# Attention: the product with the reciprocals moves to GpSimd for twelve chunks, and the maxima change sign in another instruction

## The reference, cut to what matters

```
scores = jnp.einsum('bhqd,bhkd->bhqk', q, k) / jnp.sqrt(jnp.float32(HD))
causal = jnp.tril(jnp.ones((s, s), dtype=bool))
scores = jnp.where(causal, scores, -jnp.inf)
attn = jax.nn.softmax(scores, axis=-1)
y = jnp.einsum('bhqk,bhkd->bhqd', attn, v)
```

## Time and profile before

| | |
|---|---|
| median of 3 runs | 2291.08 us |
| the profiled execution's own time | 2291.7 us |
| its span | 2290.0 us |
| TensorE (PE) busy | 2055.6 us, 90% |
| VectorE (DVE) busy | 1624.2 us, 71% |
| ScalarE (ACT) busy | 1080.5 us, 47% |
| GpSimd (POOL) busy | 715.7 us, 31% |
| attention stage | about 988 to 1720 us of the span |

### The profile page before, as it was taken

How to read it: one execution, slowest core, us unless ns; L and a number is a source line. 1 busy time by engine, 2 the same in 40 slices (tenths; PEclk the granted TensorE clock), 3 DMA queues, 4 the chain that set the end, 5 groups by cost and what they waited for, 6 DMA issues and landing times. The chain is left out here.

```text
span 2290.0 us, 41749 instructions
## 1 busy us (share of the span) xinstructions
PE 2055.6 (90%) x17396; PEld 1211.0 (53%) x17396; DVE 1624.2 (71%) x2564; ACT 1080.5 (47%) x1060; POOL 715.7 (31%) x494
## 2 busy tenths in 40 slices
PE   7899999999995999989998898898992499999998
PEld 3554444444442445544444444444431499999997
DVE  7789999999976566667778778778567544444442
ACT  6688898898861233213434444444430222323331
POOL 3410000000002112325676767767541222222211
PEclk9999999999997999959999999999996699999999
DMA  7321221221215114351022031010213444444431
GB/s 276 136 82 49 69 75 49 74 71 52 74 31 193 37 47 138 134 119 38 20 66 46 19 82 30 19 38 10 79 42 129 156 120 120 120 117 116 118 69 23
DMA packets 91961, 187.95 MB, mean 82 GB/s; under 512 B 14365, under 2 KB 23581, under 8 KB 87389
## 3 DMA queue, kind: packets, MB, share of 16 engines
q1 hardware_dynamic: 82812, 164.30, 21.9%
q0 software_dynamic: 8960, 20.98, 4.9%
HBM read 139.51 MB, written 41.28 MB: 79 GB/s over the span
## 5 line engine op out<-in xcount | busy, mean ns | idle before, releaser
L1475 ACT ACTIVATE t_E<-t_s 128x1024 f32<-128x1024 f32 (+3 forms) x320 | 278.0, 894 | 420.9 <-PE t_s L1700 231.3
L1541 DVE TENSOR_REDUCE t_rm<-t_m 128x1 f32<-128x512 f32 (+3 forms) x640 | 370.4, 603 | 139.7 <-PE t_m L1683 85.9
L615 ACT ACTIVATE m_step<-m_ub,gat_bias 128x2048 bf16<-128x2048 f32 x128 | 250.0, 1989 | 14.2 <-DMA m_ub<-scratch_uac 8.8
L757 PE MATMUL m_bd<-m_mask,m_S 128*32 128x512 bf16 x3072 | 230.3, 379 | 11.0 <-DVE m_mask L705 11.0
L757 PE MATMUL m_bd<-gat_adjT,m_S 128*32 128x512 bf16 x2496 | 201.4, 379 | 4.8 <-PE m_dn L757 4.8
L757 PE MATMUL m_bd<-m_mask,m_neg 128*32 128x512 bf16 x2496 | 188.9, 379 | 0.0
L2056 POOL DMA_INDIRECT out<-e_ye,e_token x40 | 80.9, 2024 | 338.9 <-DVE e_ye L2159 334.2
L942 POOL MEMSET k_triq<- 128x128 bf16 x1 | 0.2, 204 | 574.8 <-POOLq L2281 574.8
L2220 PE MATMUL e_h<-e_xTh,e_w1h 128*128 128x320 f32 x512 | 159.0, 311 | 1.4 <-DVE e_xTl L2140 1.4
L1714 PE MATMUL t_o<-t_E,k_rows 128*32 128x512 f32 (+3 forms) x1280 | 159.7, 573 | 0.5 <-DVE t_out L1501 0.5
L2220 PE MATMUL e_h<-e_xTh,e_w1l 128*128 128x320 f32 x512 | 158.8, 310 | 0.0
(11 more groups left out here) (371 smaller groups left out, 4414.4 us busy)
## 6 DMA issues: line engine op xcount, KB each, us to landing
a_adj<-in_adj SPq DMA_DIRECT2D x16, 1024.0 KB, 4.9
m_ub<-scratch_uac SPq DMA_DIRECT2D x16, 1024.0 KB, 4.9
e_w1r<-in_L_ffn_w SPq DMA_DIRECT2D x8, 2048.0 KB
e_w2r<-in_L_ffn_w SPq DMA_DIRECT2D x8, 2048.0 KB, 9.1
tq_Q<-scratch_parts SPq DMA_DIRECT2D x36, 256.0 KB, 4.7
gat_scale<-scratch_uac SPq DMA_DIRECT2D x32, 256.0 KB
scratch_parts<-o_hi SPq DMA_DIRECT2D x32, 256.0 KB, 2.2
scratch_parts<-o_lo SPq DMA_DIRECT2D x32, 256.0 KB, 2.7
```

The source lines that it names most:

```text
L615: act.activation(step(n), ub[h % 2][:, :].rearrange("p (t q) -> p t q", t=T), ACT.Relu, bias=bias[:, j, h:h + 1], scale=BIG).then_inc(step ...
L757: return pe.matmul(out[c * TILE:(c + 1) * TILE, :], lhs, rhs[:, c * BANK:(c + 1) * BANK], **flags)
L1475: act.activation(E[n % 3][:, two, off:BANK], ps_s[:, two, off:BANK], ACT.Exp, scale=SCALE).then_inc(exp_done[z], 1)
L1541: dve.tensor_reduce(rm[:, h, t, ch:ch + 1], ps_m[i % 2][:, 0:w], AX, ALU.max).then_inc(entry_read, 1)
```

## The change

For chunks 0 to 11 (the first three quads) GpSimd multiplies the whole of `out` by the whole of `den` in one instruction, behind its additions of step `END` + 8, when all four reciprocals of the chunk are counted; it raises `normed` by 4. VectorE keeps the reciprocals and leaves these chunks' products out. For chunks 12 to 15 it still makes them, and before the first product of a chunk it also waits until `normed` stands at the number of all chunks before. The maxima are no longer multiplied by -1 in `m`: the copy of the turned ones from PSUM into `mT` becomes a multiplication by -1, and the reduction raises `m_ready` itself.

```diff
+    PARTS, WIDE = 4, BANK // 4
+    BY_POOL = {u: u // NC * NS + END[u % NC] + 8 for u in range((QUADS - 1) * NC)}
...
+                def divide(u):
+                    pool.wait_ge(o_copied, u + 1)
+                    pool.wait_ge(inverted, PARTS * (u + 1))
+                    pool.tensor_tensor(out[u % 2][:, :], out[u % 2][:, :], den[u % 2][:, :], ALU.mult).then_inc(normed, PARTS)
+
...
+                    for u in BY_POOL:
+                        if BY_POOL[u] == n:
+                            divide(u)
...
                 def divide(u, r):
-                    if r > 0:
+                    if r > 0 and u not in BY_POOL:
                         part = slice((r - 1) * WIDE, r * WIDE)
                         dve.wait_ge(inverted, u * PARTS + r)
                         if r == 1:
                             dve.wait_ge(o_copied, u + 1)
+                            dve.wait_ge(normed, PARTS * u)
...
-                        lk(dve.tensor_copy(mT[:, :], ps_m[i % 2][0:4 * G, 0:P]))
+                        lk(dve.tensor_scalar(mT[:, :], ps_m[i % 2][0:4 * G, 0:P], -1.0, None, ALU.mult))
...
-                        lk(dve.tensor_reduce(m[:, :, :], rm[:, :, 4 * c:4 * c + 4, 0:c + 1], AX, ALU.max))
-                        lk(dve.tensor_scalar(m[:, :, :], m[:, :, :], -1.0, None, ALU.mult))
-                        dve.sem_inc(m_ready, 1)
+                        dve.tensor_reduce(m[:, :, :], rm[:, :, 4 * c:4 * c + 4, 0:c + 1], AX, ALU.max).then_inc(m_ready, 1)
```

More of the change, by code:

```diff
@@ L1501, in copy @@
                     dve.tensor_copy(out[u % 2][:, :], ps_o[:, :]).then_inc(o_copied, 1)
-                PARTS, WIDE = 4, BANK // 4
                 def divide(u, r):
-                    if r > 0:
+                    if r > 0 and u not in BY_POOL:
                         part = slice((r - 1) * WIDE, r * WIDE)
```

## The result

The changed kernel takes 2229.44 us (median of 4 runs, 2228.86 to 2237.01), the kernel before 2291.91 beside it: ratio 0.9738, 95% interval 0.9714 to 0.9763, 62 us faster. The forecast of 2249 had the sign and the mechanism right and a third of the gain too little; the time lies 2.6 us under the range.

The account below looks back on a forecast made before the run. TensorE was taken as the bound, stalled by VectorE's reductions, with VectorE held by GpSimd's additions. Gains of 9 (quad 0), 14.5 each (quads 1, 2) and 4.5 (quad 3) sum to 42.5: 2291.7 to 2249 us, range 2232 to 2273.

Parts of the forecast that it names:

- Idle time of a middle quad: TensorE's idle time in quad 2, summed over its stretches: 10.2 of 17.9 us saved, 7.7 remaining.
- The stall before the turn: TensorE's 2.00 us wait at the transposition of the maxima in quad 2: falls to about 1.1 us.
- the 1.50 us one: TensorE's second stall in 1372.3 to 1391.9, ended by the cast behind a 1.97 us multiplication: goes.
- The clock: Middle quad: 17.3 us at half speed, full speed would save 8.6; half of that taken, 4.3 us.
- The sum over two edits: VectorE loses 53.2 us of products and 15.6 us of sign changes; gains over all quads sum to 42.5 us.
- Quad 3: Only chunk 11's products and one long sign change: 4.5 us gained; later multiplications stay on VectorE and stay held.
- The wait that I had costed there: VectorE's first multiplication of quad 3 waits for GpSimd's last: costed at nothing, at most under 4 us, once.
- Quad 0: Half the multiplication time but the same five stalls in its last third: 6.5 us idle and 2.5 clock, 9.
- GpSimd's 15.4 us at nothing: Twelve added GpSimd multiplications, 15.4 us, cost nothing; lag of 0.2 us over one four-step group; upper end 15.4 us.
- the scores don't wait for the maxima's transfers: SP's store of the product goes ahead of chunk 2's maxima: store time unchanged, 2 us of slack kept, cost nothing.
- The copy with the sign isn't held: Copy of the maxima out of PSUM: takes the cast's price, 264 ns, zero added; upper end 13 us.
- deeper one: Rival, chance 0.12: nearly all idle behind divisions goes and every low-clock stretch rises, 59 us, 2233.

Follow-up runs that it names:

- The experiment that put back 5 of the 11 to 12 us of idle: The changed kernel with two more reductions of the same block in front of each chunk's maxima: 2271.97 us, ratio 0.9886.
- The one with a single reduction more: The changed kernel with one more reduction of the same block in front of each chunk's maxima: 2256.57 us, ratio 0.9835.
- the kernel with fourteen products: The changed kernel with GpSimd also making the products of chunks 12 and 13, in quad 3: 2221.43 us, ratio 0.9659.
- the kernels with the stalls put back: The changed kernel with two more reductions in front of each chunk's maxima, 2271.97 us, and with only one more, 2256.57 us.

## Why the prediction was wrong in size

- **Idle time of a middle quad**, "10.2 of 17.9 us" saved: 11.2 and 12.4, 3 us over the forecast in the two quads together. Right, a little small. The stall before the turn fell from 2.00 to 1.04 as forecast ("about 1.1"), and the 1.50 us one went.
- **The clock**, "as the 2.00 us stall keeps over half its length, I take half: 4.3 us". This is the step that failed. Measured 10 and 7 us, 8.4 us more than forecast in the two quads together: with the stalls halved all low stretches but one left them. I had let the low clock go down in the proportion in which the stall did. The experiment that put back 5 of the 11 to 12 us of idle brought nearly all of the low clock back with them, and 7 to 8 us of time in each quad beyond the idle. The one with a single reduction more put back 2.3 us of idle, a fifth, and some 18 us at 1.2 GHz in one quad but 6 in the other. So the clock follows the stalls, but not in proportion, and by which rule stays open.
- **The sum over two edits.** I costed products and sign change by their own stalls and added. They are not additive: 0.4% and 1.6% alone, 2.6% to 3.0% together, because GpSimd's product lengthens the hold of the sign changes that stay in SBUF beside it (2.23 to 5.18 us, and 0.87 to 3.65). In this change both went together, so the sum came out too small and not too large. That the whole difference of 0.6 to 1.0% is this hold was not measured.
- **Quad 3**, 4.5 us: 2.1. I wrote that its multiplications "stay held" and took their price as unchanged. The first was held 3.67 us where the longest before was 2.52. The wait that I had costed there was innocent.
- **Quad 0**, "6.5 of its 17.4 us idle and 2.5 of clock: 9": 8.1, but 7.5 of it is idle, and the clock gave nothing (0.86 and 0.85). The number is right partly by luck: the kernel with fourteen products ran the same instructions there in 186.10 us.
- **GpSimd's 15.4 us at nothing**, with a lag of 0.2 us over a full-width group: right, with room for as much again. That the scores don't wait for the maxima's transfers: right. A new wait of 1.37 us stands in quad 3, for the transfer of the finished chunks that the shorter steps 22 and 23 no longer cover.
- **The copy with the sign isn't held**: right, 265 ns in the mean over 15 and none of all 16 over 279, with GpSimd at work beside 15 of them. The rule of the Trainium skill in VectorE: DVE Perf Modes, on Mode 2x_2P, that an operand in PSUM keeps an instruction out of the two-port mode, agrees with it; that row was missing when I forecast.
- **The rivals.** The "deeper one", 2233 with a chance of 0.12, came nearest: its 59 us were 62. But only half of its mechanism happened. The low stretches of quads 1 and 2 rose but for one. Yet 5.4 us of idle stayed in each of these quads (the forecast had left 7.7), quad 0 kept its low clock, and quad 3 got a lower one; so that its sum is so near is partly luck. The time lay under the range because I ended it at that rival's value and gave that value no width.
- **What the traces don't hold.** Of the 20 us over the forecast some 12 are in the traces (16 more in quads 1 and 2, 1 less in quad 0 and 2 less in quad 3); 8 lie between the profiled execution and the median of the changed kernel.

The Trainium skill, GPSIMD Engine Reference, Engine selection, would have products on VectorE. It has GpSimd about twice as slow with two inputs. Undisturbed that fits one product of 512 columns: 1.28 us on GpSimd against 0.68, the shortest of the 16 on VectorE in the kernel that makes them so; against four of 128 it is only 1.28 to 1.12. The kernel with one product of 512 columns on VectorE stays at 0.9792 against 0.9738 and 0.9701, so here the rule doesn't decide.

## What to carry to other kernels

Where GpSimd works without a pause, look for short VectorE instructions that take far longer than their fastest copy, and ask first which of them sits in front of a turn that TensorE waits for: moving one sign change of 16 columns into a copy out of PSUM was worth 1.6%, four times as much as moving all the products without it. What is put on GpSimd can lengthen the hold of such instructions that stay on VectorE between SBUF operands (here the sign changes; reciprocals and reductions weren't held), so move or convert all of them together. And price a stall of TensorE with its clock: here 5 us of stalls in a quad cost 12 to 13.

## What the runs showed of the hardware

A held VectorE instruction is usually let through at the end of the GpSimd instruction beside it: in the kernel before none took over 2.6 us, with additions of 2.4. But holds of 3.65, 5.18 and 3.67 us went over the ends of several GpSimd instructions and ended with the last of an unbroken row. In the kernel with fourteen products stands the longest of all, over the end of the part of quad 3 above. It costs little: while it lasts TensorE is busy 6.15 of 6.92 us, at a clock of 1.00.

```profile
1542.80 6.92 DVE L1560 TENSOR_SCALAR k_rows<-k_X,k_mv,k_inv 128x512 f32<-128x512 f32 x1 [0.25 <-DVE t_mT L1546]
```

Taking GpSimd's product away ends the long holds at the turns, which is shown, and the one in quad 3 too: there the longest product took 2.49 us. But a product on GpSimd isn't enough for a long hold. In the kernels with the stalls put back GpSimd pauses 0.36 and 0.61 us behind the product of chunk 11, and VectorE's first product of quad 3 takes 0.83 and 0.84 us. In the kernel that makes each product twice GpSimd doesn't pause behind the second, at 1501.53, until 1509.74, and still this product takes 0.45 us:

```profile
1505.48 0.45 DVE L1525 TENSOR_TENSOR t_out<-t_out,t_den 128x128 f32<-128x128 f32 x1
```

Why VectorE gets in at one end of an addition and not at another is open. In quad 2 of the kernel before it got it within an unbroken row of four additions too, as these two lines show, of VectorE and GpSimd:

```profile
1434.98 1.54 DVE L1513 TENSOR_TENSOR t_out<-t_out,t_den 128x128 f32<-128x128 f32 x1
...
1429.27 9.49 POOL L1305 TENSOR_TENSOR k_X<-k_X,t_E 128x1024 f32<-128x1024 f32 x4
```

The product ends at 1436.52, where the third of the four is over, and not at 1438.76. No run separates the two cases.
